# One stack image a pair in place of two, and two transfers of constant rows in place of nine, in a kernel of convolution, attention and a quantised layer

## What is computed

```
x = x + _L0_conv_ref(_gn(x), weight_coord, radius, weights)   # depthwise 11 x 11 convolution
t = _to_tokens(x)                                             # 16 x 256 tokens x 96
t = t + _L1_attn_ref(_ln_t(t), w_attn, w_proj)                # causal, 6 heads of 16, rotary
t = t + _L1_ffn_ref(_ln_t(t), W1, b1, W2, b2)                 # 96 -> 384 -> 96, signs as weights
x = _from_tokens(t, x)
```

## Time and profile before

| | |
|---|---|
| median of 3 runs | 279.45 us (278.8 to 280.39) |
| the profiled execution's own time | 276.62 us |
| its span, first to last instruction | 274.7 us |
| busy PE / DVE / ACT / POOL | 227.3 / 202.3 / 136.8 / 112.6 us |
| mean granted clock of TensorE | 0.928 of 2.4 GHz |
| share of the DMA queue of SP in the work of 16 DMA engines | 33.3% |

### The profile page before, as it was taken

One profiled execution on the slowest core, in us unless ns is written; L12 is line 12 of the kernel. 1 busy time (PEld: TensorE's weight loads), 2 busy tenths in 40 slices (PEclk: granted clock), 3 DMA queues, 4 the chain that ended last, 5 costly groups with the idle time before them and its releaser, 6 DMA issues.

```text
span 274.7 us, 5248 instructions
## 1 busy us (share of the span) xinstructions
PE 227.3 (83%) x1718; PEld 169.4 (62%) x1718; DVE 202.3 (74%) x514; ACT 136.8 (50%) x308; POOL 112.6 (41%) x143
## 2 busy tenths in 40 slices
PE   6487497988785976979899988969999779999990
PEld 5467486977665864656576766747775525555550
DVE  3858539999994558954788877867565968988966
ACT  1421316766570446336578756847684616145260
POOL 1201125745652344347448654395636453110102
PEclk9659989999996899566999999999999999999998
DMA  4941522787796869001445443000000000101103
GB/s 125 253 158 51 170 67 70 139 150 126 147 138 125 138 123 95 4 0 45 106 100 101 89 90 89 2 3 0 4 2 0 1 2 0 43 2 44 43 0 100
DMA packets 27548, 20.25 MB, mean 74 GB/s; under 512 B 3969, under 2 KB 26882, under 8 KB 27522
## 3 DMA queue, kind: packets, MB, share of 16 engines
q1 hardware_dynamic: 25920, 18.64, 33.3%
q10 hardware_dynamic: 1602, 1.29, 2.0%
HBM read 6.03 MB, written 1.57 MB: 28 GB/s over the span
## 4 chain that ended last, share of the span: by engine, by line
PE 46%; DVE 11%; SPq 9%; issue 7%; ACT 3%; DMA 2%; POOL 1%; DVEq 0%; POOLq 0%; ACTq 0%
PE bank L1778 7%; PE bank L1659 7%; SPq L435 6%; PE bank L1602 5%; PE bank L1539 5%; DVE nmax L1105 4%; SPq L402 3%; PE bank L1570 3%; PE bank L1461 3%; PE bank L1605 2%; DMA pt_ring<-xs_ring 2%; PE bank L1450 2%; PE bank L1551 2%; PE bank L1643 1%; PE bank L1627 1%
## 5 line engine op out<-in xcount | busy, mean ns | idle before, releaser
L1105 DVE TENSOR_REDUCE nmax<-bank 128x3 f32<-128x384 f32 x64 | 45.4, 751 | 18.8 <-PE bank L1539 18.7
L762 ACT ACTIVATE pt_ring<-bank 128x384 f32<-128x384 f32 x96 | 42.0, 491 | 13.7 <-PE bank L1572 12.9
L560 POOL TENSOR_SCALAR_AFFINE_SELECT pt_ring<-pt_ring 128x512 f32<-128x512 f32 x48 | 30.9, 648 | 36.1 <-ACT pt_ring L762 36.1
L517 POOL TENSOR_TENSOR parts<-rest_ring,parts 96x512 bf16<-96x512 f32 x16 | 20.8, 1299 | 30.1 <-ACT parts L694 30.1
L1439 PE MATMUL bank<-xs_ring,toep 128*128 128x192 f32 x144 | 29.3, 352 | 1.2 <-DVE xs_ring L971 1.2
L1439 PEld LDWEIGHTS bank<-xs_ring,toep 128*128 128x128 f32 x144 | 26.4, 208 | 2.8 <-issue 2.1
L1539 PE MATMUL bank<-stack 128*128 128x128 bf16 (+1 forms) x288 | 24.4, 233 | 4.2 <-DVE nmax L1105 2.4
L1539 PEld LDWEIGHTS bank<-stack 128*128 128x128 bf16 (+1 forms) x288 | 19.1, 105 | 10.2 <-issue 7.0
L1570 PE MATMUL bank<-stack 97*128 97x256 bf16 x96 | 23.9, 284 | 0.5 <-ACT pt_ring L762 0.5
L1778 PE MATMUL bank<-parts,w_b 128*96 128x512 f32 (+1 forms) x60 | 23.1, 492 | 1.5 <-issue 1.3
L1659 PE MATMUL bank<-parts,w_b 97*128 97x256 f32 (+1 forms) x60 | 23.2, 500 | 0.0
(11 more groups left out here) (151 smaller groups left out, 489.0 us busy)
## 6 DMA issues: line engine op xcount, KB each, us to landing
stack<-parts SPq DMA_DIRECT2D x96, 96.0 KB, 3.6
stack<-in_const SPq DMA_DIRECT2D x9, 192.0 KB, 3.3
pt_ring<-xs_ring SPq DMA_DIRECT2D x14, 120.0 KB, 3.3
tok<-in_x_tok SPq DMA_DIRECT2D x4, 384.0 KB, 7.6
out<-xs_ring SPq DMA_DIRECT2D x4, 288.0 KB, 2.6
stack<-in_x ACTq DMA_DIRECT2D x2, 384.0 KB, 8.5
stack<-nmax_t SPq DMA_DIRECT2D x32, 1.5 KB
pt_ring<-xs_ring SPq DMA_DIRECT2D x14, 36.0 KB, 2.6
```

The source lines that it names most:

```text
L517: nc.gpsimd.tensor_tensor(part(b, 2), rest_ring[:, u], part(b, 1), ALU.subtract).then_inc(s_p2, 1)
L560: nc.gpsimd.affine_select(out=v, in_=v, compare_op=ALU.is_ge, fill=0.0, base=0, pattern=[[0, 2], [0, 2], [1, P]], channel_multiplier=-1).t ...
L762: nc.scalar.activation(pt_ring[:, b % 2, h, :], bank[:, 3 + h % 2, 0:T + P], ACT.Exp, scale=float(HD) ** -0.5).then_inc(s_exp, 1)
L1105: last = nc.vector.tensor_reduce(nmax[:, b % 2, k:k + 3], bank[:, 0:3, first:first + (t + 1) * P], op=ALU.max, axis=AX.X, negate=True)
```

## The change

The stack images move by their place in SP's list, and the constant rows come in two DMAs. The first of these (slots 0 to 5) stands before the loop, and the second (slots 6 to 8) after it. In the loop, turn `j` from 3 on issues one image, that of batch `j - 3`. Images 5 and 6 follow after the loop, image 7 after `max_row(0)` and image 8 after `max_row(1)`. The wait for `s_xn` is made once, ahead of the second DMA of constants. The semaphore is split in two: PE waits for the first at L1731, and for the second at the first scores of batch 6.

```diff
-            def causal(slot):
-
-                words = stack[KROWS:P, slot, :, :, :].rearrange("p h s n -> p h (s n)").bitcast(F32)
-                sp.dma_start(words, const[KROWS:P, N_CONST:N_TABLE].unsqueeze(1).broadcast_to([P - KROWS, HEADS, T])
-                             ).then_inc(s_causal, 16)
+            def causal(first, last):
+
+                words = stack[KROWS:P, first:last, :, :, :].rearrange("p r h s n -> p (r h) (s n)").bitcast(F32)
+                table = const[KROWS:P, N_CONST:N_TABLE].unsqueeze(1)
+                sp.dma_start(words, table.broadcast_to([P - KROWS, HEADS * (last - first), T])).then_inc(s_causal[first > 0], 16)
...
-                if b >= 6:
-                    sp.wait_ge(s_xn, PAIRS)
...
+            causal(0, 6)
             for j in range(2, PAIRS):
                 join_xs(j)
-                for slot in range(2 * (j - 2), min(2 * (j - 1), RING)):
-                    causal(slot)
-                for b in (2 * j - 7, 2 * j - 6):
-                    if b >= 0:
-                        stack_image(b)
+                if j >= 3:
+                    stack_image(j - 3)
+            sp.wait_ge(s_xn, PAIRS)
+            causal(6, RING)
+            stack_image(5)
+            stack_image(6)
             max_row(0)
+            stack_image(7)
             max_row(1)
+            stack_image(8)
             for b in range(2, B):
...
+                    if b == 6:
+                        pe.wait_ge(s_causal[1], 16)
...
-            pe.wait_ge(s_causal, 16 * RING)
+            pe.wait_ge(s_causal[0], 16)
```

More of the change, by code:

```diff
@@ L246, in build @@
         s_grid = sem("s_grid")
-        s_causal = sem("s_causal")
+        s_causal = [sem(f"s_causal{i}") for i in range(2)]
         s_qzero = sem("s_qzero")
```

## The result

The changed kernel takes 268.29 us, the median of 4 runs (267.82 to 269.98), beside 279.12 us for the kernel before. The ratio is 0.9615, with a 95% interval of 0.956 to 0.967. The forecast was 270.9, a ratio of 0.969. So it is faster, by 10.8 us where 8.55 were forecast. The profiled execution took 268.04 us with a span of 266.1 us. The forecast for "an execution like the profiled one" was 268.1 with a span of 266.15.

A forecast was written before the change was run, and what follows sets the result against it. SP's DMA issues were taken to bound pairs 5 to 7 of stage A. Gains of 0.67 + 6.10 + 1.78 = 8.55 us, with images and constants costing nothing, gave 279.45 - 8.55 = 270.9 us; 80% range 266 to 275.

The forecast's parts named there:

- SP is the bottleneck of pairs 5 to 7: Stage A: SP's 20 issues a turn take some 13 to 14 us, while DVE's pace is 9.62 us a pair.
- The new order on the old clock: Stage A: with one image a turn, joins 5 to 7 have 3 to 6 us to spare, so PE's three waits go.
- SP waiting for DVE at L402 in every turn: Sign expected in the changed profile: at the joins SP catches up and waits for DVE's data; a turn's issues take 7.8 us.
- The sum of 8.55 us: PE's timeline, pairs 5 to 7: gains of 0.67, 6.10 and 1.78 us, with all pairs charged at 9.62 us.
- Images 5 to 8: After join 7: the later images delay nobody and cost nothing; `max_row(1)`'s wait covers image 7 with 1.7 us over.
- The constants: Ahead of join 2: the 1152 KB transfer takes 4.1 us (bounds 4.1 to 19.8) and is hidden, at no cost.
- join 2 lands by 38 or 39: Pair 2: behind the large transfer, join 2 lands by 38 or 39 us, before PE uses it at 41.26.
- can't overtake: SP's queue: by ring order join 2 must wait behind the 1.18 MB transfer; loss of 9 to 10 us if slow, chance 0.06.
- The passage to stage B: From 108 to 130 us: granted clock 0.61 of full; it might become worse (273 to 276 us) or better (266 to 268).
- the better rival: Passage from 108 to 130 us: PE might run at 2.4 GHz, gaining 3 to 5 us, total 266 to 268; chance 0.16.
- worse rival: Passage from 108 to 130 us: half clock or a late `max_row(1)` gives back 2 to 5 us, total 273 to 276; chance 0.12.
- The distance of 2.8 us: Median of runs (279.45 us) over the profiled execution, in an unseen part; assumed to stay the same after the change.

The follow-up runs named there:

- second profile of the changed kernel: The changed kernel run once more with nothing altered: 269.14 us (6 runs), ratio 0.9625 to the kernel before.
- third profile of before: The kernel before run once more with nothing altered, for one more profiled execution: that execution took 279.64 us.

## Why the prediction was right, step by step

**SP is the bottleneck of pairs 5 to 7.** Right, and shown from both sides: taking issues away removes the waits, and adding issues with hardly any bytes restores them.

**The new order on the old clock.** Joins 5, 6 and 7 were forecast to start at 61.0, 70.6 and 80.2 and started at 61.55, 70.33 and 79.98. Image 0 was held by its data and started at 48.65 (forecast 48.95). Of the signs that I named, "SP waiting for DVE at L402 in every turn" held only ahead of join 6. And the 3.3 us for a landing was a median, not a limit: joins landed after up to 3.9 us in the kernel before and 4.0 in the changed one. The room was enough for both.

**The sum of 8.55 us.** Right for the profiled execution: the first stretch of the two profiles is 8.83 us shorter, and the span 8.6. The pace of 9.62 us a pair, charged for all pairs, held to 0.02. That the span agrees to 0.1 us is partly luck, since later stretches gave and took microseconds (below). As the worth of the change in other executions the sum is too small: it measured 8.1 to 12.1 us there.

**Images 5 to 8.** `max_row(0)` was issued at 99.13 (forecast 99.7), image 7 at 100.84 (101.3). `max_row(1)` came at 105.96, when image 7's issues had just ended (105.92). Its data was ready at 105.26, so here SP was late by 0.7 us, where I had 1.7 us to spare: one of image 7's six issues took 1.72 us, and the data itself was 1.6 us earlier than forecast. PE's first matmul on a row maximum came at 107.90, 9.96 earlier than in the earlier trace rows, so no loss shows.

**The constants.** This term was mis-sized. I took 291 GB/s from the one microsecond in which two such transfers were at their height, and multiplied it out. It gave 4.1 us, and 6.8 with the token loads; the transfer landed after 11.2 us, and after 8.8 with little but a join beside it, which is 134 GB/s (1.18 MB / 8.8). So the 4.1 us were half of what they should have been. The answer "hidden, at a cost of nothing" was right by 0.1 to 0.2 us. The step "join 2 lands by 38 or 39" was wrong: it landed from 39.1 to some 41 us. A mean over whole landings would have been the better row: 3.3 us for 192 KB with its neighbour overlapping it, though times six (19.8 us) it was too high. The Trainium skill's fit in "DMA: Bandwidth & Descriptors", section "Anatomy of one DMA — SWDGE (gpsimd) path", gave an estimated 4.7 us, and the measured 8.8 us don't agree with it either; the fit is for another path than SP's. What the same page says of order in a ring does agree: join 2 landed after 6.9 to 8.7 us behind the transfer, and in 1.8 to 2.3 us ahead of it. My "can't overtake" went further: a transfer of join 2 did land 0.5 us before the constants.

**The passage to stage B.** In the profile the granted clock there rose, as the better rival had it. The 22 us from 99.45 on, the place of the earlier trace rows moved by 8.55:

```profile
99.45:121.45 22.00, 15.83 (x146) 10.33 (x145) 15.80 (x23) 12.30 (x31) 11.30 (x15) 0.92 0.55 97
```

The clock is 0.92 there where the earlier trace rows had 0.61. The first transposes of stage B's outputs (L1622) are reached at 119.92, 10.97 us before its place at 130.89 in the kernel before. But 2.4 us of this went back, mostly in two later stretches with a lower clock (0.74 from 168 to 172 us, 0.64 from 208 to 212), and the span kept 8.6. In the second profile of the changed kernel the passage was slow, at 0.69, and the span was 266.4 all the same:

```profile
98.00:120.00 22.00, 18.04 (x137) 12.55 (x135) 14.94 (x21) 11.35 (x31) 10.44 (x14) 0.69 0.71 88
```

So neither the better nor the worse rival describes the kernel; both describe an execution.

**The distance of 2.8 us** between profile and median, kept as it was, is the step that failed. It was 2.5 us for the kernel before and 0.25 for the changed one. The forecast for the profiled execution was right to 0.1 us, and the one for the median was 2.6 us too high. What I carried over as a part outside the change was, in the trace near the median, a larger brake: 12.1 us and not 9.0.

## What to carry to other kernels

Count the issues of a queue as work: most DMAs cost SP 0.4 to 0.7 us here, 128 bytes as well as 1152 KB, and a turn of 20 issues set the pace of a stage in which every computing engine was quicker. To see whether a queue or the DMA engines are the limit, add tiny transfers in one run and bytes in another, and look at when the transfers start as well as at how long they take to land. Take more than one profile of the kernel before: the same brake cost 8.1 us in one execution and 12.1 in another. When a large transfer is hidden by a wait of another engine, the next improvement may take that cover away, so put it behind whatever is urgent even if it costs nothing today.

## What the runs showed of the hardware

An issue by SP is not of fixed length. Most issues of images and joins took about 0.6 us, but now and then one took 1.0 to 2.5 us, in every kernel. These are the issues of the images in the kernel before:

```profile
L435 SPq DMA_DIRECT2D stack<-parts x54: 596/610/1727, 48.9 to 105.5; - x54
```

In the run with more bytes there was such an issue in every turn (1.8 to 1.9 us, DMA engines 0.85 busy), and in the kernel before two from 44 to 108 us (1.65 and 1.73). But the run with tiny DMAs had one too (1.34 us, at 88.2), in a stretch in which the engines were 0.29 busy, so load alone doesn't explain them, and what makes them stays open.

While images, joins and the added DMAs moved, mostly within the chip's memory and in pieces of 512 bytes for the images and the added ones, the rate was 132 to 155 GB/s with the engines 0.85 to 0.90 busy. The constants, in pieces of 1 KB, moved at 179 GB/s with all of them at work.

The lower level of TensorE's clock came after quite different waits. Behind 1.88 us in pair 7 of the run with more bytes the four matmuls took 1.47 us, behind 2.42 in pair 5 of the third profile of before 0.89, and behind 3.88 in pair 6 of the second 1.26. At the higher level they take 0.81. A wait of 2 us may thus cost 2 us or nearly double that, and its length alone doesn't tell which.
